# A transformer stack of eight stages: two 16-head attentions whose scores are made twice in one-pass products, without transposes

## The reference

```python
x = x + tanh(g_xattn[0]) * L0_xattn(layernorm(x), ctx, mask, ...)   # stage 0: 16 heads of 8
x = x + tanh(g_ffn[0])   * L0_ffn(layernorm(x), ...)                # stage 1: 16 experts, 4 of them per token
x = x + tanh(g_xattn[1]) * L1_xattn(...)                            # stage 2: one head, gated
x = x + tanh(g_ffn[1])   * L1_ffn(...)                              # stage 3: weights quantised to 8 bits, low-rank addition
x = x + tanh(g_xattn[2]) * L2_xattn(...)                            # stage 4: 8 heads of 64
x = x + tanh(g_ffn[2])   * L2_ffn(...)                              # stage 5: 8 experts, 2 of them per token, one shared
x = x + tanh(g_xattn[3]) * L3_xattn(layernorm(x), ctx, ctx, ...)    # stage 6: 16 heads of 8
x = x + tanh(g_ffn[3])   * L3_ffn(layernorm(x), ...)                # stage 7: 64 experts, 6 of them per token
# the attentions of stages 0 and 6, for one batch (stage 0 alone has a mask of keys):
#   q, k, v = x Wq + bq, ctx Wk + bk, ctx Wv + bv, in 16 heads of 8
#   probs = softmax(q k^T / sqrt(8));  y = concat(probs v) Wo + bo
```

## Times and profile before

| what | value |
|---|---|
| three runs, median | 595.21 us |
| three runs, lowest and highest | 591.88 and 597.31 us |
| profiled execution, span | 594.0 us |
| its mean granted TensorE clock | 0.989 |
| TensorE busy | 566.0 us (95% of the span) |
| VectorE, ScalarE, GpSimd busy | 64%, 65%, 41% |

### The profile page before, as it was taken

One profiled execution on the slowest core, in us unless ns is written; L12 is line 12 of the kernel. 1 busy time (PEld: TensorE's weight loads), 2 busy tenths in 40 slices (PEclk: granted clock), 3 DMA queues, 4 the chain that ended last, 5 costly groups with the idle time before them and its releaser, 6 DMA issues.

```text
span 594.0 us, 10687 instructions
## 1 busy us (share of the span) xinstructions
PE 566.0 (95%) x3685; PEld 410.5 (69%) x3689; DVE 381.8 (64%) x736; ACT 384.2 (65%) x781; POOL 243.2 (41%) x229
## 2 busy tenths in 40 slices
PE   8999998999999997999799999999999999999997
PEld 6567766787664775777555556577668788888885
DVE  1678865756741647777454666478838666666665
ACT  4277776755666447888675656677875566666663
POOL 5006673485014100111015681000024788888884
PEclk8999998999989999999989999999999999999999
DMA  8300001161000000000000102000001666666650
GB/s 253 144 2 2 2 1 33 20 168 47 7 2 1 0 1 1 1 2 1 2 0 1 40 14 67 1 2 1 2 5 42 163 171 174 184 173 180 183 132 35
DMA packets 14850, 33.54 MB, mean 56 GB/s; under 512 B 2912, under 2 KB 8432, under 8 KB 14672
## 3 DMA queue, kind: packets, MB, share of 16 engines
q1 hardware_dynamic: 14800, 32.89, 19.5%
HBM read 32.03 MB, written 0.85 MB: 55 GB/s over the span
## 4 chain that ended last, share of the span: by engine, by line
PE 76%; DVE 8%; ACT 7%; issue 6%; POOL 2%; DMA 1%; ACTq 0%; DVEq 0%; SPq 0%; POOLq 0%
PE bank L845 9%; PE bank L847 9%; PE bank L846 9%; PE bank L728 5%; PE bank L739 5%; PE bank L754 3%; PE bank L687 3%; ACT wa L1418 2%; PE bank L702 2%; PE bank L650 2%; PE bank L644 2%; PE bank L1253 2%; PE bank L1128 2%; PE bank L1142 2%; PE bank L1117 1%
## 5 line engine op out<-in xcount | busy, mean ns | idle before, releaser
L504 POOL TENSOR_TENSOR h_lo<-wc,h_hi 128x512 fp32r<-128x512 f32 x54 | 70.0, 1300 | 13.7 <-ACT h_hi L1487 13.7
L845 PE MATMUL bank<-xn_hi,w_hi 128*128 128x512 f32 x168 | 66.0, 393 | 3.4 <-DVE xn_lo L1975 3.1
L847 PE MATMUL bank<-xn_hi,w_lo 128*128 128x512 f32 x168 | 65.4, 390 | 0.0
L846 PE MATMUL bank<-xn_lo,w_hi 128*128 128x512 f32 x168 | 65.4, 389 | 0.0
L1964 DVE TENSOR_TENSOR wb<-arena,bank 128x512 f32<-128x512 f32 x64 | 44.0, 687 | 33.0 <-PE bank L847 33.0
L1487 ACT ACTIVATE h_hi<-wc 128x512 fp32r<-128x512 f32 x54 | 34.0, 633 | 37.6 <-DVE wc L1972 27.9
L496 POOL TENSOR_TENSOR w_lo<-ring,w_hi 128x384 fp32r<-128x384 f32 x42 | 42.7, 1019 | 19.1 <-ACT w_hi L1464 19.1
L1746 DVE TENSOR_TENSOR wa<-bank,row_max 128x512 f32<-128x512 f32 x64 | 44.3, 691 | 7.5 <-ACT wb L1364 4.3
L1364 ACT ACTIVATE wb<-wa 128x512 f32<-128x512 f32 x64 | 40.1, 630 | 13.7 <-DVE wa L1746 13.3
L1742 DVE TENSOR_REDUCE row_max<-bank 128x4 f32<-128x512 f32 x64 | 43.6, 682 | 5.9 <-PE bank L728 5.4
L1370 ACT ACTIVATE wc<-bank 128x512 f32<-128x512 f32 x64 | 38.0, 593 | 8.4 <-PE bank L739 7.8
(11 more groups left out here) (351 smaller groups left out, 1392.2 us busy)
## 6 DMA issues: line engine op xcount, KB each, us to landing
arena<-comb_rows SPq DMA_DIRECT2D x64, 256.0 KB, 4.1
ring<-in_experts SPq DMA_DIRECT2D x42, 192.0 KB, 2.5
ring<-in_experts SPq DMA_DIRECT2D x8, 256.0 KB, 4.0
mats<-in_mats SPq DMA_DIRECT2D x1, 1472.0 KB, 10.5
mats<-in_mats SPq DMA_DIRECT2D x1, 832.0 KB, 6.7
mats<-in_mats SPq DMA_DIRECT2D x2, 320.0 KB, 8.2
x<-in_x_t SPq DMA_DIRECT2D x1, 512.0 KB, 4.7
context<-in_ctx_t SPq DMA_DIRECT2D x1, 512.0 KB, 5.0
```

Source lines behind the costliest of these rows:

```text
L504: nc.gpsimd.tensor_tensor(h_lo[:, v % 3, :], hidden_of(v), h_hi[:, v % 3, :].bitcast(f32), ALU.subtract).then_inc(m_h_lo, 1)
L845: mm(out, w, x_, start=start, stop=False)
L846: mm(out, w, x_rest, start=False, stop=False)
L847: return mm(out, w_rest, x_, start=False, stop=stop)
```

## The change

- The rows of k and q are f32r, the format of one-pass products. Each head's 8 dimensions stand three times in its group of 32 partitions (`spread_columns` copies twice as often, 24 columns a time). VectorE splits them: `rows_split` multiplies the raw rows with a column that is 1 on one of the three copies and 0 elsewhere, rounds to f32r, and subtracts that from the raw rows. k then holds rounded, rest, rounded; q holds rounded, rounded, rest; so a product gives rounded·rounded plus the two products with a rest. There are 8 splits for k and 8 for q in each attention.
- Scores are made twice. First with queries on partitions, only for their maxima: VectorE reduces 1024 elements at a time (`largest`). TensorE transposes the maxima, VectorE adds them into the row TOP_ROW of `q_rows` (`take_tops`), where k has -1. Then `turned_scores` makes the scores again with keys on partitions, the maximum taken off. ScalarE makes exp from PSUM, 1024 elements at a time, straight into the operands of probs·V.
- The subtraction, the four transposes of a unit and the copy of their results are gone.
- The mask comes into the k rows by one more product into the same bank.
- In the first attention the largest weight, the scale of the quantisation and a memset of `comb_pieces`, which VectorE did ahead of the attention, stand between the batches (`beside0`).
- In stage 5, VectorE has two k splits ahead of the norm, two behind it and ahead of routing, four behind routing and ahead of the shared expert's product. The q splits of the first half stand ahead of each attention, those of the second in its first two batches.

The core of the diff:

```diff
-        k_rows = arena[:, 8192:12288].rearrange("p (g t) -> p g t", g=QUADS)
-        q_rows = arena[:, 12288:16384].rearrange("p (g t) -> p g t", g=QUADS)
+        k_rows, q_rows = (nc.alloc_sbuf_tensor_at(name, [P, QUADS, T], f32r, offset=arena_at + 4 * at)
+                          for name, at in (("k_rows", 8192), ("q_rows", 12288)))
+        K_REST, Q_REST, MASK_ROW, TOP_ROW = 1, 2, 24, 25
...
                 for g in range(2):
-                    nc.gpsimd.tensor_copy(dst[:, :, g, :, 0:HD], wide[:, :, g, :, :]).then_inc(w_spread, 1)
+                    for e in range(2):
+                        thrice = dst[:, :, g, e, 0:3 * HD].rearrange("p m (c d) -> p m c d", c=3)
+                        nc.gpsimd.tensor_copy(thrice, wide[:, :, g, e, :].unsqueeze(2).to_broadcast([P, 4, 3, HD]))\
+                            .then_inc(w_spread, 1)
...
             # TensorE
+                def by_pair(out_bank, left, right, b, p):
+                    for m_ in range(QUADS):
+                        for r in (2 * p, 2 * p + 1):
+                            rows = slice(32 * r, 32 * r + 32)
+                            last = mm(bank[out_bank + r % 2][:, m_ * P:m_ * P + P],
+                                      left[rows, m_, b * P:b * P + P], right[rows, m_, b * P:b * P + P],
+                                      start=True, stop=True)
+                    return last
                 def scores(b, p):
...
+                    by_pair(0, q_rows, k_rows, b, p).then_inc(a_s, 1)
+                def turn_tops(b):
+                    pe.wait_ge(a_max, 2 * (tb + b) + 2)
                     if b > 0:
+                        pe.wait_ge(a_exp, 2 * (tb + b) - 1)
+                    nc.tensor.transpose(bank[2][:, 0:P], top_wide[:, :], ident[:, :]).then_inc(a_top, 1)
+                def turned_scores(b):
+                    pe.wait_ge(a_taken, tb + b + 1)
+                    if b == 0:
+                        pe.wait_ge(a_q_raw, 8 * inst + 8)
+                    else:
+                        pe.wait_ge(a_exp, 2 * (tb + b))
                     for m_ in range(QUADS):
+                        for r in range(4):
                             rows = slice(32 * r, 32 * r + 32)
+                            ins = mm(bank[2 + r][:, m_ * P:m_ * P + P], k_rows[rows, m_, b * P:b * P + P],
+                                     q_rows[rows, m_, b * P:b * P + P], start=True, stop=True)
+                            if m_ == QUADS - 1 and r % 2 == 1:
+                                ins.then_inc(a_st, 1)
-                def transposes(b, u):
...
                 scores(0, 0)
+                q_rows_of(inst, 1, range(0, 2))
                 scores(0, 1)
+                q_rows_of(inst, 1, range(2, 4))
                 for b in range(B):
+                    turn_tops(b)
+                    if b + 1 < B:
+                        scores(b + 1, 0)
+                    if b >= 2:
+                        turn_back(b - 2)
+                    if b >= 1:
+                        probs_v(b - 1, 1)
+                    if b >= 2:
+                        through_o(b - 2)
+                    turned_scores(b)
+                    if b + 1 < B:
+                        scores(b + 1, 1)
+                    if b >= 1:
+                        turn_o(b - 1)
+                    probs_v(b, 0)
...
             # ScalarE
-                    fn(wb[:, u % 2, :], wa[:, u % 2, :], ACT.Exp, scale=scale).then_inc(a_exp, 1)
+                    fn(probs[p][:, :, :], banks[:, 2 + 2 * p:4 + 2 * p, :], ACT.Exp, scale=SCALE_A).then_inc(a_exp, 1)
-                def evac(b, u):
...
             # VectorE
+            def rows_split(dst, raw, rounded, rests, done):
+                link(v.tensor_scalar(rounded.bitcast(f32r), raw, rest_cols[:, rests - 1:rests], None, ALU.mult))
+                v.tensor_tensor(dst, raw, rounded, ALU.subtract).then_inc(done, 1)
...
+                def largest(b, p):
...
+                    v.tensor_reduce(tops, banks[:, 0:2, :].rearrange("p r (m k) -> p r m k", m=QUADS), X, ALU.max)\
+                        .then_inc(a_max, 1)
+                def take_tops(b):
+                    dve.wait_ge(a_top, tb + b + 1)
+                    part = q_rows[:, :, b * P:b * P + P]
+                    v.tensor_tensor(part, bank[2][:, 0:P].unsqueeze(1).to_broadcast([P, QUADS, P]), part.bitcast(f32),
+                                    ALU.add).then_inc(a_taken, 1)
...
+                for b in range(B):
+                    take_tops(b)
+                    if b + 1 < B:
+                        largest(b + 1, 0)
+                        if b < 2:
+                            q_rows_split(inst, 4 + 2 * b)
+                        largest(b + 1, 1)
+                        if b < 2:
+                            q_rows_split(inst, 5 + 2 * b)
+                    beside(b)
+                    if b >= 1:
                         divide(b - 1)
...
+            def beside0(b):
+                if b in (0, 1):
...
+                    v.tensor_reduce(w_max[:, b:b + 1], ffn_weights(b), X, ALU.max, apply_absolute_value=True)\
+                        .then_inc(d_rowmax, 1)
+                if b == 2:
+                    dve.wait_ge(d_max, 1)
...
+                    v.tensor_scalar(w_neg, w_scale, -1.0, None, ALU.mult).then_inc(d_scaled, 1)
+                if b == 3:
+                    v.memset(comb_pieces[:, :, :], 0.0)
...
+            for n in range(2):
+                k_rows_split(1, n)
             norm(NORM_OF[5][0])
+            for n in range(2, 4):
+                k_rows_split(1, n)
...
             pick()
+            for n in range(4, 8):
+                k_rows_split(1, n)
...
             norm(NORM_OF[6][0])
-            attn(1)
+            for n in range(4):
+                q_rows_split(1, n)
+            attn(1, lambda b: None)
```

More of the change, by code:

```diff
@@ L378, in beyond, with k_raw @@
             return not isinstance(b, int) or b >= k
+        probs = (wb, wc)
+        def k_raw(inst, n):
+            return far_raw[:, n % 6, :] if inst else near_raw[:, n % 4, :]
         def hidden_of(v):
@@ new lines, in probs_v, with turn_o @@
+                    for e in range(2):
+                        for m_ in range(QUADS):
+                            h = 8 * p + 2 * m_ + e
+                            last = mm(bank[6][32 * m_:32 * m_ + 32, p * P:p * P + P],
+                                      v_ones[:, b, 32 * h:32 * h + 32], probs[p][:, e, m_ * P:m_ * P + P],
+                                      start=(e == 0), stop=(e == 1))
+                    last.then_inc(a_pv, 1)
+                def turn_o(b):
+                    pe.wait_ge(a_ocopy, tb + b + 1)
+                    if b > 0:
+                        pe.wait_ge(update_ready, u_count(A_STAGE[inst]) + b)
+                    for g in range(2):
+                        last = nc.tensor.transpose(bank[7][:, g * P:g * P + P], o_sb[:, g, :], ident[:, :])
+                    last.then_inc(a_turned, 1)
@@ L1401, in units @@
-                exp(0, 0)
-                over_batches(act, batch)
+                    act.wait_ge(a_y, tb + b + 1)
+                    update(s, y, before + b if before + b > 0 else None, P)
+                for b in range(B):
+                    if b >= 2:
+                        copy_back(b - 2)
+                    if b >= 1:
+                        copy_o(b - 1)
+                    if b >= 2:
+                        batch_update(b - 2)
+                    exp(b, 0)
+                    exp(b, 1)
@@ L1772, in divide @@
                         .then_inc(a_norm, 1)
-                def extra(b, u, odd):
-                    if u == 3 and beyond(b, 1):
+                largest(0, 0)
+                largest(0, 1)
+                for b in range(B):
+                    take_tops(b)
[7 more added lines that the diff above has]
+                    beside(b)
+                    if b >= 1:
                         divide(b - 1)
-                units(base, extra)
                 if inst == 0:
```

298 lines of the change are left out of this document (122 added, 176 removed).

## The result

The changed kernel takes 613.33 us (median of 4 runs, 610.89 to 614.86) against 594.1 of the kernel before on the same chip: ratio 1.0316, interval 1.0268 to 1.0363. It is 3.2% slower. The forecast was 585.5, with a range of 578 to 597; the profiled execution has a span of 611.9 against 594.0, at a mean granted clock of 0.897 where it was 0.989.

A forecast was written before the change was run, and what follows sets the result against it. TensorE was taken to bound the kernel, being the wall in both attentions. Terms -6.5 + 6.2 + 1 - 10.5 = -9.8 gave a span of 584.2; with 1.2 added for the median, 585.5 us, range 578 to 597.

The forecast's parts named there:

- Prices of the new instructions: Both attentions and splits: exp of 1024 elements 1.05 us, largest-of-1024 1.21, taking maxima 0.69, split 1.15.
- The one-pass step: Score products in both attentions: one one-pass product over 32 rows and 128 columns takes 0.11 us.
- four-pass pace: Rival, chance 0.20: in the attentions a score step takes 0.22 us, not 0.11; 5.3 per batch, 590 us in all.
- row groups one after another: Rival, chance 0.08: one-pass products of different 32-row groups don't run side by side; 6.4 us per batch, 601 to 603.
- The circle of 4.6 us: Attention loop: waits from exp through probs·V, maxima, scores, Wo and turned scores back to exp, 4.6 us against 6.8.
- The lower clock: Rival, chance 0.05: waits in the circle halve TensorE's clock in the attentions; circles of 8.2 us, 622 in all.
- GpSimd as the first attention's new wall: First attention: GpSimd's quantisation steps, from about 51.8 us, set its end at 84.2 against 90.6, so -6.5.
- Stage 5: Stage 5: eight k splits on VectorE delay routing and the shared expert's product, +6.2 us, plus 1 for the clock.
- the lower clock behind it: Stage 5: a TensorE idle for five us may come back at a lower clock, +1 us, bounds 0 and 2.
- Second attention: Second attention: scores begin at 377.6 us, first addition at 396.4, end at 426.7 against 437.2, so -10.5.

The follow-up runs named there:

- no fill: Changed kernel with the quantisation's scale known ahead of the second batch and stage 5's splits moved into VectorE's waits, no idle products added: 608.93 us.
- the start filled: Changed kernel plus idle fp32 products in TensorE's waits from ahead of the first scores to the third batch of both attentions: 599.38 us.
- the scale early: Kernel of "the start filled" with the quantisation's scale known ahead of the second batch and GpSimd's steps spread otherwise: 583.23 us.

## Why the prediction was wrong, point by point

- **Prices of the new instructions**: right, each within 0.1 us. The one-pass step was the bold one; a score block of four steps takes 0.59 from start to start at 2.4 GHz, 0.64 forecast. The rival *four-pass pace* was wrong, and so was *row groups one after another*.
- **The circle of 4.6 us**: right, 4.54, but only where the clock is 1.00. In the changed kernel it is 7.12, and made of TensorE alone.
- **The failing step** is the one that set the clock aside: both attentions were priced at 2.4 GHz throughout. *The lower clock* stood as a rival at 0.05, on the ground that a stretch with TensorE busy 4.14 of 6.0 us kept 1.00. That row is of another loop, with other products, and says nothing on this one. Here the clock falls in the first three batches, which I had counted as VectorE's and then as harmless to TensorE; and I asked only whether waits in the *new* circle would lower it, not what a loop does once it is low. Shown: it falls behind those waits (no fill: 608.9 us), it is held in the second attention when they are filled with dense products (1.00 in five kernels), the steady loop does not lift it once fallen (36.00 of 36.00 us busy at 0.50; only in a last batch did it rise by itself), and dense or four-pass products do. It is the whole miss in the second attention (62.6 us for 49.1), and about 9.7 of the 13.2 in the first, whose last addition with dense products in every batch came at 87.69 (forecast 84.2). The rival's own price, 622, came from circles of 8.2; they are 7.1.
- **GpSimd as the first attention's new wall**: right in kind, hidden by the clock. With the clock lifted by dense products in every batch its row of steps ran without a gap. GpSimd's timeline of that kernel, first step and last addition:

```profile
55.34 1.57 POOL L555 TENSOR_SCALAR diag<-mats,w_stat 128x512 f32<-128x512 f32 x1
...
87.69 0.45 POOL L587 TENSOR_TENSOR x<-x,upd 128x128 f32<-128x128 f32 x1
```

32.35 us, forecast 32.4 (27.7 + 2.0 + 2.7). It began 3.5 late, at 55.3: partly the clock, partly a term that I did not have (below).
- **Stage 5**: +8.6, forecast 7.2. The four splits ahead of the shared expert's product, the last of them and that product in VectorE's timeline after, and TensorE's wait for it:

```profile
317.79 0.48 DVE L1770 TENSOR_SCALAR arena<-arena,rest_cols 128x512 fp32r<-128x512 f32 x1
...
321.67 0.69 DVE L1771 TENSOR_TENSOR k_rows<-arena 128x512 fp32r<-128x512 f32 x1
322.28 1.28 DVE L2201 TENSOR_TENSOR wc<-wb,bank 128x512 f32<-128x512 f32 x2
```

```profile
323.01 2.07 PE L1247 MATMUL bank<-wc,mats 128*128 128x512 f32 x2 [4.38 <-DVE wc L2201]
```

From 317.79 to 322.28 is 4.5 us, forecast 4.6. Counted from the stage's first `select` (290.35 before, 296.88 after), routing ended 1.9 later, as forecast (1.3 + 0.6), and TensorE's product came 6.0 later (310.52 before, 323.01 after; forecast 6.2). The row at 324 to 328 above is the lower clock behind it, forecast at 1 with bounds of 0 and 2: about 2.6, what is left of 8.6. This term was mis-sized. The Trainium skill's rule on the shared port ("SBUF — State Buffer", SBUF: two separate sides), by which such a subtraction and a GpSimd instruction exclude each other, agrees with what moving the splits cost: 1.64 for 0.69.
- **Second attention**: it began 2.0 later, as forecast, and its additions, by source line, span as much as in the earlier trace rows:

```profile
L580 POOL TENSOR_TENSOR x<-x,upd x8: 455/456/457, 414.2 to 455.5; 128x128 f32 x8
```

41.3 us from first to last, 41.1 before: at half clock the work taken away saves nothing. The first addition came 18.1 later than before, 17.3 of it from ahead; forecast 18.8 behind the first scores, it was 21.3, the last of these batches being at half clock already.

What stays open: why the clock fell at 60 us in one kernel and not in another with the same waits there; which of the waits between 30 and 42 us is the one that tips it, and whether the five idle products that the change dropped would have been enough there; and why it rose in the last batch of some attentions and not of others. No kernel held the clock from start to end of both attentions with the changed kernel otherwise as it was.

## What to carry to other kernels

Removing TensorE work in a loop can also remove what keeps its clock up. Ask for each stretch that gets waits whether it can fall there, and then what the loop behind it does at the lower level: if that loop's products are short and one-pass, price it at 1.2 GHz to the stage's last batch. A few dense idle products in waits that exist anyway cost nothing on the path (4.54 us per batch with two of them in each, 4.53 without), eight per batch did (5.87). Here they decided whether the change pays: 608.9 without them, 582.5 and 579.4 with them, 594 for the kernel before.

## What the runs showed of the hardware that was not expected

- A TensorE that is busy in every microsecond can stay at 1.2 GHz for 36 us. Busy time in the profile is no sign of the clock; the granted clock has its own column.
- In the second attention the same loop held 2.4 GHz for 20 us if it started there (416 to 436 above) and 1.2 GHz if it started there: two paces of one program, 4.53 and 7.12 us per batch. In the first attention it did not always hold: the clock fell at 62 in that kernel, at 60 with the start filled, and held with the scale early.
- The instruction behind a partition all-reduce on GpSimd started some 7 us late in each kernel where no longer wait hid it. GpSimd's timeline of the kernel after, and a row of the second instruction's line:

```profile
47.97 0.38 POOL L583 PARTITION_ALL_REDUCE w_max<-w_max  x1 [36.90 <-DVE w_max L2093]
55.59 0.44 POOL L587 TENSOR_TENSOR x<-x,upd 128x128 f32<-128x128 f32 x1 [7.24 <-issue]
...
L587 POOLq MODIFY_POOL_CONFIG  x2: 82/82/83, 48.3 to 48.3; - x2
```

The update that the addition at 55.59 needs was ready at 51.1, and the row puts its idle time down to the engine's own issue. The all-reduce's result was not late: in the kernel before, VectorE's scale, which waits for it, began at 28.92, 0.04 behind its end. Between the two stand two MODIFY_POOL_CONFIG instructions on GpSimd's sequencer, which kernel.py does not write; with the scale early they stand behind the all-reduce too (34.3). That they are what takes the 7 us is likely, but not shown. With the scale early the step behind the same all-reduce (33.99) began at 41.04, with 6.67 put down to issue, though the scale that it needs was done at 37.1. In the kernel before any such delay lay under a wait of 19 us. Moving that instruction into the loop put it in front of the first addition.
